# FFN weight codes made inside the attention passes, and the residual handed over in tiles of 128 tokens

## The reference

```
x = x + tanh(g_xattn[0]) * latent_attention(layernorm(x), ctx)     # 16 heads, rope
x = x + tanh(g_ffn[0])   * quantised_ffn(layernorm(x))
x = x + tanh(g_xattn[1]) * causal_attention(layernorm(x), ctx)
x = x + tanh(g_ffn[1])   * routed_ffn(layernorm(x))                # 7 experts, 2 chosen, 1 shared
```

```
scale = mean(abs(w)) + EPS;          wq = clip(round(w / scale), -1, 1)
s = max(abs(x), per token)/127 + EPS; xq = clip(round(x / s), -128, 127)
y = (xq @ wq.T) * s * scale          # gate: silu(y_gate) * y_up, then quantised again, then down
```

## Time and profile before

| what | us |
|---|---|
| median of 3 runs | 2117.43 (2115.23 to 2124.33) |
| the profiled execution | 2123.64, its span 2121.9 |
| PE busy, share of span | 1877.3 (88%) |
| DVE busy | 1428.5 (67%) |
| ACT busy | 944.4 (45%) |
| POOL busy | 669.6 (32%) |

### The profile page before, as it was taken

The page is one execution under the profiler, slowest core; times in us unless marked ns, Lnnn a source line. Parts: engine busy times, 40 slices in busy tenths (PEclk is TensorE's granted clock), DMA queues, the critical chain, the costliest instruction groups (busy, mean ns, idle before and its releaser), DMA issues. The chain is left out here.

```text
span 2121.9 us, 31624 instructions
## 1 busy us (share of the span) xinstructions
PE 1877.3 (88%) x11466; PEld 1489.5 (70%) x11466; DVE 1428.5 (67%) x2714; ACT 944.4 (45%) x1971; POOL 669.6 (32%) x620
## 2 busy tenths in 40 slices
PE   4899999999999999999427998899868899999997
PEld 4677778877678877777314554666545789999996
DVE  5777776778776777776677777477645535666664
ACT  3433333444433344433483332555425236666663
POOL 4322222226421222221113000232222464555553
PEclk9999999999999999999758999899978999999999
DMA  4111001110101110100321000000022347777774
GB/s 194 37 37 37 7 31 37 37 37 31 67 6 37 37 37 37 37 1 1 159 90 59 0 0 0 1 1 2 1 76 100 103 87 209 238 237 234 235 234 87
DMA packets 31106, 153.59 MB, mean 72 GB/s; under 512 B 5468, under 2 KB 5468, under 8 KB 20084
## 3 DMA queue, kind: packets, MB, share of 16 engines
q1 hardware_dynamic: 19268, 128.33, 16.6%
q0 software_dynamic: 11408, 23.37, 6.0%
q10 hardware_dynamic: 288, 0.00, 0.0%
HBM read 131.17 MB, written 20.51 MB: 71 GB/s over the span
## 5 line engine op out<-in xcount | busy, mean ns | idle before, releaser
L263 POOL TENSOR_TENSOR la_q_roped<-la_q_roped 128x400 f32<-128x400 f32 x128 | 132.6, 1056 | 668.4 <-DVE la_q_roped L683 668.4
L588 ACT ACTIVATE la_probs<-banks,la_minus_max 100x361 f32<-100x361 f32 x256 | 144.5, 564 | 196.5 <-DVE la_minus_max L736 196.5
L683 DVE TENSOR_TENSOR la_q_roped<-banks,la_rope_q 128x400 f32<-128x400 f32 x384 | 196.8, 566 | 30.9 <-PE banks L386 15.1
L1877 DVE TENSOR_TENSOR ex_weights_low<-ex_raw_weights,ex_weights_high 128x2048 fp32r<-128x2048 f32 x60 | 137.6, 2294 | 51.4 <-ACT ex_weights_high L1772 48.8
L423 PEld LDWEIGHTS banks<-identity,la_probs 100*121 100x121 f32 x768 | 113.1, 184 | 70.8 <-DVE la_probs L743 44.7
L743 DVE TENSOR_SCALAR la_probs<-la_probs,la_rsum 100x361 f32<-100x361 f32 x256 | 154.1, 602 | 9.1
L1030 PE MATMUL banks<-qf_sign_weights,qf_x_quant_t 128*100 128x512 bf16 x512 | 122.2, 389 | 33.0 <-DVE qf_hidden L1111 18.6
L434 PE MATMUL banks<-la_probs_t,la_kv_rows 121*128 121x200 f32 x768 | 151.3, 332 | 0.0
L736 DVE TENSOR_REDUCE la_minus_max<-banks 100x1 f32<-100x361 f32 x256 | 135.0, 527 | 16.2 <-PE banks L414 9.6
L423 PE MATMUL banks<-identity,la_probs 100*121 100x100 f32 x768 | 126.0, 273 | 21.2 <-DVE la_probs L743 18.3
L2144 POOL TENSOR_TENSOR ex_g_low<-ex_g,ex_g_high 128x256 fp32r<-128x256 f32 (+1 forms) x104 | 86.5, 948 | 180.9 <-ACT ex_g_high L1816 180.5
(11 more groups left out here) (321 smaller groups left out, 5370.7 us busy)
## 6 DMA issues: line engine op xcount, KB each, us to landing
ex_raw_weights<-w_exp SPq DMA_DIRECT2D x60, 1024.0 KB, 4.9
la_weights<-w_pack SPq DMA_DIRECT2D x15, 1856.0 KB, 7.6
qf_raw_weights<-w_ffn SPq DMA_DIRECT2D x2, 4096.0 KB, 22.0
residual<-x SPq DMA_DIRECT2D x2, 2048.0 KB, 14.7
qf_raw_weights<-w_ffn SPq DMA_DIRECT2D x2, 2048.0 KB
out<-ex_block_out POOLq DMA_DIRECT2D x13, 256.0 KB, 4.0
normed_rows<-ex_xn SPq DMA_DIRECT2D x16, 200.0 KB
out<-residual SPq DMA_DIRECT2D x4, 800.0 KB
```

The lines of the kernel that those rows point to most:

```text
L263: pool.tensor_tensor(roped[:, h, 0, c, :], roped[:, h, 0, c, :], roped[:, h, 1, 1 - c, :], ALU.add).then_inc(b_add, 1)
L588: act.activation(prob[:, s % 4, 0:L], ps[0:S, s % 2, 0:L], ACT.Exp, bias=nmax[:, s % 4:s % 4 + 1], accum_out=sums[:, s % 4:s % 4 + 1]).the ...
L683: dve.tensor_tensor(roped[:, h, v, c, :].rearrange("p (b s) -> p b s", b=GB), ps[:, B_BANKS[k % 2], 0:NT].rearrange("p (b s) -> p b s", b=GB),
L1877: dve.tensor_tensor(wl[:, m, :], raw[:, m, :], wh[:, m, :].bitcast(F32), ALU.subtract).then_inc(w_low[m], 1)
```

## The change

**Weights.** The block that quantises them is gone. The three matrices are cut into 33 chunks of 128 x up to 768 float32 (384 KB). Two buffers of the latent attention, `turned` and `trigk`, hold the chunks in turn. In passes 1 to 6 ACT sums absolute values, six chunks a pass, the last three in pass 6. In pass 7 the scales are made. In passes 9 to 14 each chunk is loaded again, ACT scales and rounds it, DVE clips and subtracts into the one bf16 buffer `signs`, and SyncE stores it to DRAM (`w_quant`), again six a pass and three in pass 14. Each engine's chunks stand at fixed places in the front of the pass: ACT's 0 and 1 first, 2 ahead of the copy `high(n, 3)`, 3 to 5 between it and the copy of the rank; DVE's between the ropes. SyncE waits for the chunks of a pass before it loads the weights of the next. The rope table in `trigk` is loaded anew after pass 6.

**Residual.** x goes to DRAM (`x_mid`) in batches and comes back in 13 tiles of 128 tokens (`x_all`; the last has 64), so that a tile uses all partitions. The statistics of the first six tiles are computed in passes 14 and 15. After the tiles x goes through DRAM again (`x_next`) back into the layout by batches.

**FFN.** One block, all tiles unrolled. SyncE loads the bf16 codes, 2 MB a matrix, with the last packed tiles between them. Only four tiles of x are normalised, rounded and transposed ahead; for the others this is done inside the tile loop, four ahead: POOL normalises and scales, DVE finds maximum and scales (`x_scales`) and rounds (`x_quantise`), TensorE transposes, ACT copies (`x_turned`). The new statistics are no longer taken behind the add of each tile: those of batches 0 to 7 in steps 7, 8, 11 and 12, the rest in the causal attention, of the last four batches within its slots 4 to 9. POOL splits the attention weights after its last rounding.

The core of the diff:

```diff
@@ latent_attention, sync
+                def refill_sums(n):
+                    ...
+                    for c in chunks_of(n, FIRST_SUM):
+                        if c + 2 < len(chunks):
+                            sp.wait_ge(q_abs, c + 1)
+                            load_chunk(c + 2)
+                def refill_signs(n):
+                    for c in chunks_of(n, FIRST_SIGN):
+                        m, lo, width = chunks[c]
+                        sp.wait_ge(q_done, c + 1)
+                        sp.dma_start(w_quant[m, :, lo:lo + width], signs[:, 0:width]).then_inc(q_out, 16)
+                        if c + 2 < len(chunks):
+                            load_chunk(c + 2)
+                for n in range(2, RUNS + 1):
+                    refill_sums(n - 1)
+                    refill_signs(n - 1)
...
                     sp.wait_ge(k_psum, (n - 1) * UNITS)
...
@@ latent_attention, scalar
+                def chunk(n, k):
...
+                        act.wait_ge(q_in[c % 2], loads_of(c, again))
+                        if again:
+                            act.activation(w, w, ACT.Identity, bias=rnd[:, 0:1],
+                                           scale=core.winv[:, m:m + 1]).then_inc(q_up, 1)
+                        else:
+                            act.activation(w, w, ACT.Abs, accum_out=wsum[:, m, c % CM:c % CM + 1]).then_inc(q_abs, 1)
                 def pair(n):
+                    chunk(n, 0)
+                    chunk(n, 1)
                     high(n, 2)
+                    chunk(n, 2)
                     high(n, 3)
+                    chunk(n, 3)
+                    chunk(n, 4)
+                    chunk(n, 5)
...
                     rank_out(n, 0)
@@ latent_attention, vector
+                def chunk(n, k):
...
+                    dve.wait_ge(q_up, c + 1)
+                    dve.tensor_scalar(w, w, ROUND - 1.0, ROUND + 1.0, ALU.max, ALU.min).then_inc(q_clip, 1)
+                    dve.wait_ge(q_clip, c + 1)
+                    if c:
+                        dve.wait_ge(q_out, 16 * c)
+                    dve.tensor_scalar(signs[:, 0:width], w, ROUND, None, ALU.subtract).then_inc(q_done, 1)
                 def pair(n):
                     rope(n, 0, 0)
                     rope(n, 0, 1)
                     rope(n, 0, 2)
                     low(n, 2)
+                    chunk(n, 0)
                     rope(n, 1, 0)
                     rope(n, 1, 1)
+                    chunk(n, 1)
                     rope(n, 1, 2)
                     low(n, 3)
+                    chunk(n, 2)
+                    if n == RUNS - 2:
+                        core.wait_packed(dve, 0)
+                        for t in core.packed[0]:
+                            dve.bn_stats(core.stats_all[:, t, :], core.x_all[:, t, :]).then_inc(x_bn, 1)
...
                     rope(n, 2, 0)
+                    chunk(n, 3)
                     rope(n, 2, 1)
+                    chunk(n, 4)
                     rope(n, 2, 2)
+                    chunk(n, 5)
@@ quantised_ffn, vector
+                for t in range(PT):
+                    widen(t)
+                    if t + FIRST < PT:
+                        x_scales(t + FIRST)
+                    if t:
+                        add(t - 1)
+                    quantise(t)
+                    if t + FIRST < PT:
+                        x_quantise(t + FIRST)
+                    for g, steps in enumerate(((7, 8), (11, 12))):
+                        if t in steps:
+                            dve.wait_ge(core.rows_in[g], 16 * GB)
+                            ...
@@ quantised_ffn, scalar
+                for t in range(PT):
+                    for c in range(NC - 1):
+                        widen(t, c)
+                    if t:
+                        turn(t - 1)
+                        if t + FIRST - 1 < PT:
+                            x_turned(t + FIRST - 1)
+                    widen(t, NC - 1)
```

More of the change, by code:

```diff
@@ L200, in latent_attention, with chunks_of, loads_of @@
         KV_BANKS = (T_BANK, V_BANK)
+        def chunks_of(n, first):
+            return range(max(0, (n - first) * EACH), max(0, min(len(chunks), (n - first + 1) * EACH)))
+        def loads_of(c, again):
+            return 16 * (c // 2 + 1 + (again and (len(chunks) + 1 - c % 2) // 2))
         def starts_half(n):
@@ L1064, in _ @@
[L1064 to L1068 removed]
+                    if t:
+                        narrow(t - 1)
+                turn(PT - 1)
+                narrow(PT - 1)
             @block.scalar
             def _(act):
[L1072 to L1074 removed]
@@ L1095, in _ @@
-                own_scale(0, 0)
-                for c in range(NC):
-                    widen(0, 0, c)
-                tile(1, 1)
-                with act.Fori(0, B // 2 - 1) as i:
-                    for par in range(2):
-                        tile(i * 2 + par + 2, par)
-                turn(B - 1, 1)
+                        if t >= 2:
+                            act.wait_ge(o_psum, t - 1)
+                        act.copy(hqt[:, t % 2, half * (IC // 2):(half + 1) * (IC // 2), 0:n], pst(half, n)).then_inc(t_out, 1)
@@ new lines, in _ @@
+                lo = core.packed[1][0]
+                root(0, lo, 0)
+                act.wait_ge(consts, 2)
+                for t in range(FIRST):
+                    n = rows_of_tile(t)
+                    act.wait_ge(n_inv, t + 1)
+                    act.activation(xn[0:n, t % XB, :], xn[0:n, t % XB, :], ACT.Identity, bias=rnd[0:n, 0:1],
+                                   scale=xinv[0:n, t:t + 1]).then_inc(n_mul, 1)
+                    if t:
+                        x_turned(t - 1)
+                root(lo, PT, PT - lo)
@@ L1157, in quantised_ffn @@
+                add(PT - 1)
     return wa
```

589 lines of the change are left out of this document (337 added, 252 removed).

## The result

The change makes the kernel a little slower: 2130.81 us, median of 8 runs (2129.31 to 2135.03), against 2117.09 for the kernel before on the same chip. The ratio is 1.0054, 95% interval 1.0038 to 1.0070. Measured again with the later experiments the ratio was 1.0037 (1.0021 to 1.0053), run 11. The prediction was 2110 us; the range (2078 to 2142) holds the result, the sign is the wrong one.

The account below looks back on a forecast made before the run. The prediction took TensorE to bound the attention passes and a loop of dependent steps to bound the tiles. Its terms, -61 - 16 - 0.7 + 6 + 3.5 + 60 + 1, gave -7 us: 2110 us, range 2078 to 2142.

Parts of the forecast that it names:

- part 2: FFN tiles: thirteen tiles of 128, first to last fourth gated product (c3) 170.6 us instead of 186.5, -16 us.
- The period is a loop: FFN tiles: a chain from one tile's fourth gated product (c3) to the next's sets the period, 11.93 us before.
- That is +0.76: FFN tile loop: DVE's net added time per step in us, from scales and rounding less statistics and a wait.
- The periods, 13.7 and 11.7: FFN tiles: us per step, 13.7 for nine steps that still prepare a tile, 11.7 for the last three.
- Rival (c): FFN tiles: TensorE too idle to keep 2.4 GHz, period about 22 us, +100 us, kernel 2210 us; chance 0.03.
- part 1: Between attention and FFN: the weight stage goes, 26.5 to 28 us instead of 88.4, -61 us.
- part 4: Attention passes 1 to 6: ACT's sums of absolute values delay the copy of the rank, +3.5 us.
- part 3: Hand-over from the tiles to the next attention: reloaded rows, statistics and late small steps, +6 us, with -0.7 at the end.
- Part 5: Attention passes 9 to 14: in-order waits for code transfers in the front, 10.9 us a full pass, +60 us.
- Rival (a): Attention passes: the transfers are hidden, +16 us for sums and codes, kernel 2062 us; chance 0.10.
- rival (b): Passes 9 to 14: a store takes 4.0 us, a full pass loses 16.3, kernel 2140 us; chance 0.17.

Follow-up runs that it names:

- run 11: The changed kernel measured again as it is, on the chip of the experiments: 2133.02 us, ratio 1.0037 to the kernel before.
- run 5: Changed kernel with ten more matmuls, results unused, in TensorE's gap of each FFN tile step from the second on: 2124.73 us, ratio 1.0000.
- run 4: Changed kernel with the residual add moved behind the hidden state's rounding and the code chunks moved into softmax slots: 2064.55 us, ratio 0.9718.
- run 1: Changed kernel with one move, the residual add of the tile before placed behind the rounding of the hidden state: 2103.24 us, ratio 0.9913.
- run 6: Changed kernel with the six code stores of a pass issued behind its last chunk, so codes in DRAM are wrong: 2129.15 us, ratio 1.0027.
- run 2: Kernel before with one move, its residual add that of the tile just before, not two back: 2181.65 us, ratio 1.0275.
- run 8: run 4's kernel with POOL's split of the attention weights in 16 instructions of 512 columns instead of 4 of 2048: 2061.79 us, ratio 0.9704.

## Why the prediction was wrong

**The step that failed** is in part 2: "The period is a loop: c3, add, statistics, maximum ..." and the count behind it ("That is +0.76"; its terms give 0.78). It kept the add in the loop with its duration alone. The diff turns `widen(t + 2)`, `add(t)`, `quantise(t + 2)` into `widen(t)`, `add(t - 1)`, `quantise(t)`: the add is of the tile one back instead of two back. Nothing in the earlier trace rows shows a wait there, because the old distance kept it away. I had counted instructions and not asked anew what each waits for. Of the 26.7 us by which the tiles missed, 15.1 are that wait and what it moves (run 5 less run 4), 9.3 the clock that falls behind the longer gap (changed kernel less run 5), and 2.4 the rest (run 4's 173.0 against the 170.6 of the sum). The rest isn't the meetings with POOL: in run 4 they cost 8.1 us, and the sum had 8.5 for them. It lies in the two steps with the statistics and those meetings, where TensorE stands still for longer and restarts slowly (granted clock 0.79 from c3 of tile 7 to c3 of tile 9 in run 4, and DVE waits 4.11 and 3.57 us for TensorE ahead of c3 instead of 2.80 for silu); the sum had no term for that. The step costs about 3 us more outside the tiles: the hand-over is 23.9 us in the changed kernel and 20.8 in run 1. The periods, 13.7 and 11.7, were right for the order that I had in mind: run 1 has 13.57 and 11.67.

**Rival (c)** saw that the clock could fall and had the condition and the size wrong. Its condition, TensorE idle 2 us of a period of 13.7, is what run 1 has (1.92 of 13.57), and there the clock stays at 1.00. In the regular steps it fell only with the gap of 2.80 us that the add's wait makes, which no part of the prediction had. And it priced the clock as all or nothing (a period of 22 us, +100), where in every other step a part of TensorE's work ran at half speed, 9.3 us in all.

**Right, by the sum's own steps:** part 1 (27.6 us from add to c3, predicted 27; DVE's last wait for a transfer is for the queued packed tiles); part 4 (+4 in this execution, predicted +3.5; in the ten executions with this code passes 1 to 6 are 2.5 to 4.5 us longer than before in nine, and 1.4 shorter in run 1).

**Right by luck:** part 3 (+5.6, predicted +5.3). From c3 to the aggregate it took 23.9 us where the prediction's terms give 20.2, nearly all of it the add's wait again, since run 1 has 20.8; and the late statistics cost nothing where it had 3. The two errors cancel.

**Part 5: mechanism right, size a little off.** The front is set by in-order waits for transfers, TensorE waits for the copy of the rank and restarts at half speed. A full pass lost 8.6 us, not 10.9, and pass 14 6.5, not 5.5: 49.5 instead of 60. The store landed in 2.1 us, not 2.7, the load in 3.3 instead of 3.1, so that the load, not the single buffer of signs, set the pace; run 6 shows the store's wait worth 0.8 to 1.5 us a pass. In the pass shown TensorE's wait in one piece is 4.74 us, not 6. By the fit in the Trainium skill (DMA: Bandwidth & Descriptors, "Anatomy of one DMA — SWDGE (gpsimd) path"), 2.0 us plus bytes at 436 GB/s, an estimate for 192 KB is 2.45 us and for 384 KB 2.9. The trace has 2.1 and 3.3, on SyncE's queue, where the fit is for GpSimd's. Rival (a), hidden transfers, did not happen and rival (b), the slow store, neither. With the measured 49.5 in place of 60 the forecast would have been about 2100 us, further off: by luck this error hid more than a third of the error of part 2.

**The numbers.** On the profiled execution the sum was -7 and it came out +11.4: +26.8 from the tiles and -8.7 from the passes are the difference. The chance for "slower" was 0.20, of which 0.17 rested on the store and 0.03 on the clock, none on a wait in the tiles.

## What to carry to other kernels

When a change turns a software pipeline's order, write down for each instruction of the loop which tile it is of, before and after, and what it then waits for: an instruction that never waited in the old trace may do so one tile earlier, and its wait moves all that stands behind it. Put work in the engine's own gap (here between the third and the fourth product) rather than at the place where its data become ready, and put work that waits for transfers into a stretch where nobody waits behind it, with the loads of the critical path ahead of it in the queue. Price TensorE's clock by the part of the work that runs at half speed, not as all or nothing: here a gap that grew from 1.92 to 2.80 us a step cost 9.3 us in 13 tiles.

## What the runs showed of the hardware

- TensorE's granted clock stayed at 1.00 with one gap of 1.92 us in each 13.57 us (run 1) and fell in part with one gap of 2.80 us in each 14.5 or 16.1 (changed kernel, 0.94, in alternate steps) or 3.42 in 14.9 to 17.4 (run 2, 0.90, in three steps of four). Ten matmuls without use in the gap brought it back to 1.00 and made the tiles 9.3 us shorter, though each step then held 2.3 us more of TensorE's work (run 5).
- A DVE rounding of 1.2 or 1.3 us takes 2.5 to 5.5 us beside POOL instructions of 3.6 to 5.4 (changed kernel, runs 4 and 5), longest where the two begin together, and 2.2 to 2.9 us beside pieces of 1.0 to 1.7 us (run 8). Cutting POOL's work costs it little (20.0 us in 16 instructions, 18.1 in 4).
- A store of 192 KB from SyncE's queue lands in 2.1 us, six of them issued one behind another in 3.8 (median of run 6), while the one write of the earlier trace rows took 4.0 for 256 KB from POOL's.
